# Seven block products in more groups of a fused adaLN, attention and FFN kernel, and the scan work placed earlier

## What is computed

```python
def _bi_wkv(r, k, v, w, u, time_emb):
    tf = sigmoid(sum(time_emb, -1))[:, None, None]
    decay = exp(-exp(w))[None, :] * (0.5 + 0.5 * tf[:, :, 0])
    ek = exp(minimum(k, 30.0)); ekv = ek * v
    # a = a*decay + ekv_t ; b = b*decay + ek_t, forward (nf, df) and in reverse (nb, db)
    euk = exp(minimum(u + k, 30.0))
    num = nf + nb - ekv + euk * v
    den = df + db - ek + euk
    return sigmoid(r) * (num / maximum(den, 1e-08)) * (0.8 + 0.2 * tf)

def _ffn(x, W1, W2, W3):                 # B, S, D, H = 4, 512, 512, 2048
    hidden = silu(x @ W1.T) * (x @ W3.T)
    return fwht(hidden) @ W2.T

x = x + attn(_bi_wkv(x, f, f, w, u, cond), Wq, Wk, Wv, Wo, betas)
x = x + _ffn(_bi_wkv(x, f, f, w2, u2, cond), W1, W2, W3)
```

## Time and profile before

| | us |
|---|---|
| median of 3 runs (1578.01 to 1578.4) | 1578.29 |
| the profiled execution | 1582.11 |
| its span | 1580.3 |
| busy PE / DVE / ACT / POOL | 1544.1 / 1227.1 / 780.9 / 614.9 |

### The profile page before, as it was taken

How to read it: one execution, slowest core, us unless ns; L and a number is a source line. 1 busy time by engine, 2 the same in 40 slices (tenths; PEclk the granted TensorE clock), 3 DMA queues, 4 the chain that set the end, 5 groups by cost and what they waited for, 6 DMA issues and landing times.

```text
span 1580.3 us, 24552 instructions
## 1 busy us (share of the span) xinstructions
PE 1544.1 (98%) x8406; PEld 1326.8 (84%) x8406; DVE 1227.1 (78%) x2746; ACT 780.9 (49%) x1687; POOL 614.9 (39%) x433
## 2 busy tenths in 40 slices
PE   4899999999999999999999999999999999999999
PEld 2688988888888888888888888888888888888887
DVE  8879968898888788888765764666897888677785
ACT  3566656545625526544555562663554443444442
POOL 3656657252111212222001010144664466666662
PEclk9899999999999999999999999999999999999999
DMA  5366677586584486386288558247211222311111
GB/s 176 119 226 240 236 264 275 190 317 251 187 309 158 155 313 238 105 296 222 78 295 313 201 210 334 93 162 258 87 54 54 64 88 69 107 49 59 54 41 54
DMA packets 113405, 276.58 MB, mean 175 GB/s; under 512 B 11648, under 2 KB 36608, under 8 KB 111872
## 3 DMA queue, kind: packets, MB, share of 16 engines
q1 hardware_dynamic: 94416, 241.96, 42.4%
q10 hardware_dynamic: 18864, 33.04, 6.7%
HBM read 226.71 MB, written 48.25 MB: 174 GB/s over the span
## 4 chain that ended last, share of the span: by engine, by line
PE 91%; DVE 5%; issue 2%; ACT 1%; POOL 0%; DMA 0%; ACTq 0%; SPq 0%; DVEq 0%; POOLq 0%
PE psG L666 14%; PE psG L668 14%; PE psG L667 14%; PE psG L790 6%; PE psX L862 4%; PE psX L666 3%; PE psX L668 3%; PE psX L667 3%; PE psX L817 3%; PE psG L792 3%; PE psZ L843 3%; PE psZ L834 3%; PE psZ L842 2%; PE psZ L668 2%; PE psY L668 2%
## 5 line engine op out<-in xcount | busy, mean ns | idle before, releaser
L2226 POOL TENSOR_TENSOR parts<-stage,parts 128x512 fp32r<-128x512 f32 x160 | 235.6, 1494 | 136.5 <-ACT parts L1717 134.2
L666 PE MATMUL psG<-yh,parts 128*128 128x512 f32 x646 | 263.3, 408 | 0.1
L668 PE MATMUL psG<-yh,parts 128*128 128x512 f32 x646 | 253.1, 392 | 0.0
L667 PE MATMUL psG<-yl,parts 128*128 128x512 f32 x646 | 252.2, 390 | 0.0
L2294 POOL TENSOR_TENSOR vs<-v,omb 128x512 f32<-128x512 f32 x64 | 92.9, 1475 | 391.6 <-PE psX L817 214.6
L668 PEld LDWEIGHTS psG<-yh,parts 128*128 128x128 f32 x646 | 121.3, 188 | 26.6
L666 PEld LDWEIGHTS psG<-yh,parts 128*128 128x128 f32 x646 | 121.9, 189 | 22.1 <-issue 0.9
L667 PEld LDWEIGHTS psG<-yl,parts 128*128 128x128 f32 x646 | 122.0, 189 | 21.3
L790 PE MATMUL psG<-heads,parts 128*128 128x512 f32 x384 | 135.5, 395 | 0.0
L1717 ACT ACTIVATE parts<-stage 128x512 fp32r<-128x512 f32 x152 | 87.8, 622 | 50.8 <-DMA stage<-in_w 15.7
L1875 ACT ACTIVATE kT<-psG 128x512 f32<-128x512 f32 x62 | 36.9, 595 | 151.5 <-PE psG L668 150.1
(11 more groups left out here) (281 smaller groups left out, 4151.8 us busy)
## 6 DMA issues: line engine op xcount, KB each, us to landing
parts<-high_o SPq DMA_DIRECT2D x52, 512.0 KB, 6.2
parts<-low_o SPq DMA_DIRECT2D x52, 512.0 KB, 7.6
parts<-high_v SPq DMA_DIRECT2D x36, 512.0 KB, 5.1
parts<-low_v SPq DMA_DIRECT2D x36, 512.0 KB, 6.5
stage<-in_w SPq DMA_DIRECT2D x64, 256.0 KB, 3.1
parts<-high_k SPq DMA_DIRECT2D x23, 512.0 KB, 5.5
parts<-low_k SPq DMA_DIRECT2D x23, 512.0 KB, 7.2
parts<-high_q SPq DMA_DIRECT2D x23, 512.0 KB, 4.6
```

Source lines behind the costliest of these rows:

```text
L666: e.matmul(out, lh, rh, start=first, stop=False, skip_group_check=check)
L667: e.matmul(out, lh, rl, start=False, stop=False, skip_group_check=check)
L668: return e.matmul(out, ll, rh, start=False, stop=last, skip_group_check=check)
L2226: e.tensor_tensor(lo, raw, hi, ALU.subtract).then_inc(p_wl, 1)
```

## The change

**Three more fast groups.** Groups 5, 6 and 7 of the FFN's first half become fast (`FAST0` = 5, `FASTS`). Group 8 stays plain. The activations' sums T are therefore needed twice, once for batches 0 and 1 (half 0) and once for 2 and 3 (half 1). The first time T lies where the late tiles' results are (`zh2`, `zl2`, `zh3`, `zl3`), so these are first stored to DRAM (`late_s`, 4 MB in four DMAs, `z_out`) and loaded again behind group 7 (`z_back`). The four inputs of T are now put together from the high and low part (`t_part`, four additions of 128x1024), before the four subtractions (`t_sum`).

**Late tiles.** All late steps have to be done before T is written, so `shared_out_ffn` has places only in units 0 to 7 (before: 0 to 16), and `FROOM` rises from 1400, 1400, 1900, 1900 to 2900, 2900, 3300, 3300. One tile (24, batch 2's first chunk) is scanned in the attention (`NA` = 25); only its `zt` and `zl` are left for the FFN, its ratio loaded from DRAM. `ROOM` of the attention rises by 0 to 200 ns per place.

```diff
-NA = 24
+NA = 25
...
-ROOM = (600, 500, 1100, 1500, 1000, 900, 1000, 1400)
+ROOM = (600, 500, 1200, 1700, 1200, 1000, 1200, 1500)
...
+FAST0 = 5
+FASTS = list(range(FAST0, NG)) + list(range(NG + 1, 2 * NG))
+LATE_ORDER = [25, 24, 26, 27, 28, 29, 30, 31]
...
-FSTEPS = [(name, t, cost) for t in range(NA, NT) for name, cost in SCAN + LATE]
-FROOM = (1400, 1400, 1900, 1900)
-LAST_ROOM = (3500, 3500, 3500, 3500)
+FSTEPS = [(name, t, cost) for t in LATE_ORDER for name, cost in (SCAN if t >= NA else ()) + LATE]
+FROOM = (2900, 2900, 3300, 3300)
+LAST_ROOM = (3900, 3900, 3900, 3900)
...
-    for u in range(17):
+    for u in range(2 * FAST0 - 2):
...
+            def sums_of_z(half):
+
+                for place in (T1, T3, T2, T4):
+                    t_part(place, half)
+                t_sum(T1, T3, half, True)
+                t_sum(T3, T2, half, True)
+                t_sum(T2, T1, half)
+                t_sum(T4, T2, half)
...
+            def plain_unit(u, before):
...
+                half = u // (2 * NG)
+                sums = u in (2 * FAST0 - 2, 2 * NG)
                 for j in range(2):
...
                     behind_ffn(u, j)
...
+                    if sums and j == half:
+                        sums_of_z(half)
+                        s_sums("1", FAST0 if half == 0 else NG + 1)
+                if before is None:
+                    return
                 for dc in range(NC):
-                    add_x(u - 1, dc)
+                    add_x(before, dc)
...
+            def high_t(place, half, n):
+
+                w.wait_ge(v_ts, 8 * half + 4 + n)
+                if half == 0:
+                    w.wait_ge(d_zo, 64)
...
+            def z_out():
+
+                w.wait_ge(a_zh, 16)
+                w.wait_ge(v_zl, 8)
+                for r in range(4):
+                    e.dma_start(late_s[r], late_z[r][:, :, :].bitcast(F32)).then_inc(d_zo, 16)
+
+            def z_back():
+
+                i = FAST_NO[NG - 1]
+                w.wait_ge(d_zo, 64)
+                w.wait_ge(pe_3, 4 * (NG - 1) + 3)
+                e.dma_start(zl2[:, :, :].bitcast(F32), late_s[1]).then_inc(d_zb, 16)
+                w.wait_ge(pe_x, 4 * i + 3)
+                e.dma_start(zh2[:, :, :].bitcast(F32), late_s[0]).then_inc(d_zb, 16)
+                e.dma_start(zh3[:, :, :].bitcast(F32), late_s[2]).then_inc(d_z, 16)
+                w.wait_ge(pe_3, 4 * (NG - 1) + 4)
+                e.dma_start(zl3[:, :, :].bitcast(F32), late_s[3]).then_inc(d_z, 16)
...
+                elif u % 2 == 0 and g == FAST0 - 2:
+                    z_out()
+                    load_w(PLACE["3", FAST0] + 1)
+                elif u == 2 * NG - 1:
+                    z_back()
+                    load_w(PLACE["3", NG + 1] + 1)
+                    out_of(u - 1)
```

More of the change, by code:

```diff
@@ L1041, in down @@
                 m.then_inc(pe_2, 1)
-            for u in range(1, 2 * FAST[0]):
-                for k, (j, kind) in enumerate(((0, "1"), (0, "3"), (1, "1"), (1, "3"))):
+            UPS = ((0, "1"), (0, "3"), (1, "1"), (1, "3"))
+            for u in range(1, 2 * FAST0):
+                for k, (j, kind) in enumerate(UPS):
                     if u == 1:
@@ L1118, in tensor @@
                 a_z(G[1], "3", g, 0, 1, *z21, True, True).then_inc(pe_x, 1)
-                down(*before[5 if g < FAST[-1] else 4])
+                down(*before[5 if g < FASTS[-1] else 4])
                 w.wait_ge(a_sn, 6 * i + 6)
@@ L1123, in tensor @@
                 s_t(X[0], "3", g, 3, *z22, False, True).then_inc(pe_x, 1)
-                for k in range(6 if g < FAST[-1] else 5, 8):
+                for k in range(6 if g < FASTS[-1] else 5, 8):
                     down(*before[k])
@@ L1655, in vector @@
                 add_x(*before[2])
-                if not fewer:
+                if not final:
                     s_sums("1", g + 1)
@@ L2138, in high_s, with plain_unit @@
                              SR[:, :, :, :].rearrange("p k c d -> p (k c d)"), ACT.Copy).then_inc(a_sw, 1)
[L2140 to L2141 removed]
+            def plain_unit(u):
+                half = u // (2 * NG)
+                g = ffn[u][0]
+                turned = u in (2 * FAST0 - 1, 2 * NG)
+                split_hi(PLACE["2", g] + (3 if u % 2 == 0 or g + 1 in FAST_NO else 4))
                 for j in range(2):
@@ L2146, in scalar @@
                     behind_ffn(u, j)
-                    if u == 2 * NG and j == 0:
+                    if turned and j == half:
                         for n, place in enumerate((T1, T3, T2, T4)):
-                            high_t(place, n + 1)
-                        high_s("1", FAST[0])
+                            high_t(place, half, n + 1)
+                        high_s("1", FAST0 if half == 0 else NG + 1)
                 behind_ffn(u, 2)
                 behind_ffn(u, 3)
+            for u in range(1, 2 * FAST0):
+                plain_unit(u)
             def take(i, g, k, kind, bank, value):
@@ L2405, in gpsimd @@
                     behind_ffn(u, j)
-                    if u == 2 * NG and j == 0:
+                    if turned and j == half:
                         for n, place in enumerate((T1, T3, T2, T4)):
-                            low_t(place, n + 1)
-                        low_s("1", FAST[0])
+                            low_t(place, half, n + 1)
+                        low_s("1", FAST0 if half == 0 else NG + 1)
                 behind_ffn(u, 2)
                 behind_ffn(u, 3)
-            for g in FAST:
-                more = g < FAST[-1]
+            for u in range(1, 2 * FAST0):
+                plain_unit(u)
+            for g in FASTS:
+                more = g < FASTS[-1]
+                if g == NG + 1:
+                    plain_unit(2 * NG)
+                    plain_unit(2 * NG + 1)
                 low_s("3", g)
```

243 lines of the change are left out of this document (153 added, 90 removed).

## The result

The changed kernel takes 1668.86 us (1666.25 to 1670.0, 5 runs), the kernel before 1578.29 (1577.77 to 1578.82, 5 runs): ratio 1.0571, 95% interval 1.0559 to 1.0583. It is 90.6 us slower; 80 were forecast, and the time lies in the range.

The account below looks back on a forecast made before the run. TensorE's work, and whatever makes it wait, was taken to bound the kernel. The terms 72 - 8.2 + 12 + 4 gave +80 us on 1578.3, so 1658 us (own range 1636 to 1680; overall from just below 1611 to 1690).

Parts of the forecast that it names:

- The start: Start of the FFN's late steps: unit 1's gate starts at 1110.1 us instead of 1101.65; bank X waits until 1110.8.
- The pace of units 2 to 7: FFN units 2 to 7: VectorE sets the pace, about 19.3 us a unit, planned late steps stretched by 1.19.
- E: End of the last late step in units 1 to 7, put at 1244.4 us, bounds 1229.4 and 1262.
- The loads behind z_out: Ahead of unit 8's first gate: group 5's W1 and W3 loads queue behind 4.19 MB of stores, landing at E + 17.2.
- Sums and parts: Ahead of group 5: sums, weight sums and parts start the S and T product at E + 53.6 = 1298, 72 us late.
- Behind group 7: After group 7's end F: reloads, and sums ahead of `add_x` delaying `down` of unit 15; 12 us, bounds 3 and 20.
- The clock: TensorE's lower clock after two waits, for S and T and for `add_x`: 4 us; waits in units 2 to 9 free.
- The attention: One more tile scanned in the attention, 15 us real over 21 periods: taken as 0, from above 15.
- light stretching: Rival on the late steps: E = 1229.4, loads overtake the stores for free; +33 us, 1611; chance 0.22.
- "Not slower": Rival on units up to 9: TensorE's lead and VectorE's idle 18% absorb everything; 8.2 us come off, 1570; chance 0.05.
- Blocking for all of GpSimd's time: Rival on seven FFN units: every GpSimd instruction blocks VectorE throughout; 63 us lost instead of 15, +48, 1706; chance 0.05.
- The attention rival: Attention's first 21 periods: VectorE goes over 90%, holding up the segment recurrence, up to 15 us; 1673; chance 0.10.

Follow-up runs that it names:

- experiment 3: Changed kernel with the late tiles' reciprocals on 32 of 128 columns, the rest not computed: 1662.76 us, ratio 1.0534 to the kernel before.
- experiment 1: Changed kernel with the loads of group 5's W1 and W3 issued ahead of `z_out`'s stores instead of behind them: 1654.86 us, ratio 1.0486 to the kernel before.
- experiments 6 to 8: Variants with one fast group in the first half: unit 16's additions ahead of its sums, 1623.72 us; unit 12 likewise, 1623.87; then second half's sums in pieces, 1626.52.
- experiment 2: Kernel before with late steps packed as densely as in the changed one (`FROOM`, `LAST_ROOM` raised), no fast group more: 1622.47 us, ratio 1.0282.
- experiment 10: Kernel before with the changed kernel's scan steps a period in the attention (`ROOM`), no tile added: 1584.95 us, ratio 1.0043.
- experiments 2 and 11: experiment 2, and the version with one first-half fast group and unit 16's additions ahead of its sums, given the attention of the kernel before: 1625.1 us, ratio 1.0296.
- experiment 9: Version with one first-half fast group and sums behind the additions in both halves, GpSimd's low parts of T cut to 128 of 1024 columns: 1607.97 us, ratio 1.0195.

## Why the prediction was right, point by point

- **The bound, and the removed matmuls**: right. 36 matmuls less, and each new wait came at full length.
- **The start**: the gate expected at 1110.1 us came at 1108.8, and bank X was released at 1109.6 (predicted 1110.8).
- **The pace of units 2 to 7**: right in kind, wrong in its make-up. E was put at 1244.4; the last `zl` ends at 1248.7 and the additions behind it at 1249.9. VectorE was to be busy over 95% and was 89%: its waits for ScalarE, 13.4 us, were counted only as six times 0.7. It was busy for 125.5 us from the first gate to E where 130.1 were counted; less 36.3 for gates and additions that is 89.2 us for 78.8 planned, a factor of 1.13 and not 1.19. Too much work and too little waiting partly cancel. By the prediction's own sign ("if VectorE shows idle time in units 2 to 7") this step, VectorE as the only bound, is wrong in part, and experiment 3 shows the same: of 14.4 us taken off VectorE, 7.5 came off the stretch. The gates of G from unit 2 (1125.9) to unit 7 (1237.3) lie 22.3 us apart, where 19 to 20 were forecast for a unit; units 1 and 7 are shorter.
- **The loads behind z_out**: forecast for E + 17.2, they came at 1261.8, 12 us behind the measured E. The mechanism is right (experiment 1); the rate was counted too slow. The DMAs moved 368 GB/s from 1249 to 1262 us, and over 400 in most of it, where 334 was taken.
- **Sums and parts**: the second gates came 17.8 us behind the loads, where 16.5 were counted. The product with S and T was forecast at 1298, and started at 1298.6. That it comes so close is luck: E was 5 us late, and the loads came 5 us sooner behind it.
- **Behind group 7**: 12 us forecast, 15.2 measured. The wait of `down` was 13.1 for 10, and its cause is the one named, the sums ahead of the additions; but moving them does not save it (experiments 6 to 8), which the prediction did not ask. The twelve sums took 20.6 us (1409.9 to 1430.5); the prediction's own terms, five of 1.21 and seven of 2.57, make 24.0, and not the 18 or so that lead to its F + 37.5. Only five of the twelve were stretched.
- **The clock**: 4 us forecast for the two waits behind the pace-setting stretch; 10 and 12 slow matmuls there cost 2.1 and 2.4. The slow matmuls in units 2 to 9 add up to 10.8 us. That they cost nothing there, because VectorE sets the pace, stays argued: the sum below and that of experiment 2 add them to the waits, and no run shows whether the waits would be longer without them.
- **The attention**: the step that failed. It said "I take 0"; the denser steps cost 6.7 us (experiment 10). Its cover was read from two shares, VectorE 85% busy and TensorE 2.2 us idle, which say nothing of when the steps fall. In the two profiles the attention seems only 2.2 us longer (`down` of unit 0 at 1096.3 for 1094.1), because the profiled execution of before was itself slow there: two other kernels with its scan steps (experiments 2 and 11) reach it at 1089.4 and 1089.6. Experiment 10 reaches it at 1097.3 without the added tile, as late as the kernels that have it (1096.3 to 1099.9), so the tile itself shows no cost of its own.
- **The sum.** From the first `down` of unit 0 to the end, after takes 1664.4 - 1096.3 = 568.1 us and before 1580.3 - 1094.1 = 486.2, 81.9 more. Its terms: 70.4 more of waits, 15.4 of slow matmuls, -8.2 of removed ones, and some 3.5 because after each of 22 waits the first matmul also gives up its overlap with the last (0.39 - 0.23 = 0.16 each), in all 81.1. The 81.9 and the attention's 6.7 are 88.6 of the 90.6 between the medians; 2 us stay open, less than the 2.6 by which after's profiled execution lay below its median. Against the 80 of the forecast: 6.7 more for the attention, 3.2 and 0.5 more behind group 7 (its waits and the clock), 1.5 less ahead of the product with S and T, which started 202.3 us behind that `down` where 131.8 were due: 88.9.

The rivals: light stretching fell with experiment 9 and with the stores' 13.8 us. "Not slower" fell with unit 8's second gates, at 1279.6 where it needed 1219. Blocking for all of GpSimd's time was the right rule (a 0.42 us sum took 2.56) and still not the right price: the factor was 1.13 over units 1 to 7, and 2 or more for the sums in the turns that met a low part. The attention rival was right that there is a cost. Its condition didn't come (VectorE at over 90%: it was 86% from 60 to 380 us in after), and 6.7 of its 15 us did. The measured 1668.9 lies nearer to its 1673 than to the forecast's 1658, so the range is met with a term in it that was put at nothing.

## What to carry to other kernels

When an algorithm with fewer products needs sums and splits on the side engines first, price the whole chain (sums, high and low parts, what GpSimd locks while they run) against the cover in front of its first use: here 2.7 us a group stand against 11 to 13 us of wait a turn, and the three other orders tried only renamed that wait. Small loads that somebody needs soon go ahead of a large store on the same queue. And a busy share of 85% is no room: ask for the waits of a run in which only the density is changed.

## What was not expected of the hardware

- In the earlier trace rows the slow matmuls stand behind 4.27 us of idle time and not behind 2.48. In the FFN shorter waits do it too: behind 2.11 us in experiment 2 seven matmuls started 0.43 us apart, at a granted clock of 0.50, and behind 2.39 us in after six. Behind 13.13 us in after it was eleven slow starts. In after such a wait costs 1.5 to 2.7 us more than itself. But behind 3.06 and 3.18 us in after, and 2.40 in experiment 2, the pace was kept at a clock of 1.00 in after, so the length of the wait alone does not say which it will be.
- Two sums of 1.21 us took 2.32 and 2.30 beside the last of four splits of GpSimd and a low part of 128x512 behind it, which itself took 2.27 us where others took 1.29.
- The granted clock read 0.95 in the profile of before and 1.00 in that of after (1440 to 1570 us), at one and the same distance of matmul starts, 0.2267 us. Two profiles can't be compared by it at this level.
- A kernel's profiled execution can hide some 4.5 us in an early stretch: without the marks of experiments 2 and 11 the attention seemed to cost 2.2 us.
